# Three graphs of a batched graph network: earlier steps, turning by DMA, and two gathers in place of four

## The reference

```python
A = (adj != 0)
h = x
for l in range(5):
    m = h @ weight[l]
    agg = einsum('bij,bid->bjd', A, m)
    h = gru_cell(agg, h, w_ih, w_hh, b_ih, b_hh)
x = layernorm(x + h * mask)
fused = 0
for g, idx in enumerate(GROUPS):          # 25, 9, 7, 6 and 6 nodes
    h = graph_conv(x[:, idx], adj[:, idx][:, :, idx], W1[g], b1[g])
    fused[:, idx] += norm_w[g] * graph_conv(h, ..., W2[g], b2[g])
x = layernorm(x + fused)
```

## Time and profile before

| What | Value |
|---|---|
| Median of three executions | 503.38 us |
| The profiled execution's own time | 503.91 us |
| Its span, from first to last instruction | 502.2 us |
| PE busy | 486.9 us, 97% of the span |
| DVE, POOL, ACT busy | 75%, 63%, 59% |
| Mean granted TensorE clock | 0.995 of full speed |

### The profile page before, as it was taken

How to read it: one execution, slowest core, us unless ns; L and a number is a source line. 1 busy time by engine, 2 the same in 40 slices (tenths; PEclk the granted TensorE clock), 3 DMA queues, 4 the chain that set the end, 5 groups by cost and what they waited for, 6 DMA issues and landing times.

```text
span 502.2 us, 7158 instructions
## 1 busy us (share of the span) xinstructions
PE 486.9 (97%) x2313; PEld 230.8 (46%) x2313; DVE 375.8 (75%) x711; ACT 297.1 (59%) x522; POOL 318.6 (63%) x314
## 2 busy tenths in 40 slices
PE   7999999999999999999999999999989999999994
PEld 4344444444444444444444444434434444564564
DVE  3867867697857688998789878878664878545795
ACT  4546655645565666666567665566653656745564
POOL 3654775758775687776696567869652546324465
PEclk9999999999999999999999999999998999999999
DMA  8768253665525357345937565352242331322313
GB/s 276 229 166 170 44 151 66 175 114 152 146 44 168 84 120 175 83 84 124 209 72 180 146 145 146 64 104 45 42 103 43 63 69 42 63 61 43 78 44 85
DMA packets 131620, 55.44 MB, mean 110 GB/s; under 512 B 95145, under 2 KB 123262, under 8 KB 131582
## 3 DMA queue, kind: packets, MB, share of 16 engines
q1 hardware_dynamic: 106204, 31.86, 30.9%
q10 hardware_dynamic: 25378, 23.12, 15.2%
HBM read 27.70 MB, written 4.19 MB: 64 GB/s over the span
## 4 chain that ended last, share of the span: by engine, by line
PE 78%; DVE 11%; ACT 3%; issue 2%; DMA 2%; POOL 2%; SPq 1%; POOLq 0%; ACTq 0%; DVEq 0%
PE pA L757 23%; PE pR L764 6%; PE pR L762 6%; PE pR L763 6%; PE pZ L764 6%; PE pZ L763 6%; PE pZ L762 6%; PE pHN L762 3%; PE pHN L763 3%; PE pHN L764 3%; PE pIN L762 3%; PE pIN L764 3%; PE pIN L763 3%; DVE T L1354 2%; DVE T L1358 2%
## 5 line engine op out<-in xcount | busy, mean ns | idle before, releaser
L757 PE MATMUL pA<-A,NAT 128*128 128x512 fp8e4 x640 | 152.7, 381 | 0.6 <-DMA NAT<-HT 0.3
L520 POOL TENSOR_TENSOR HT<-H,HT 128x512 f16<-128x512 f32 x74 | 89.1, 1205 | 100.3 <-ACT HT L1126 100.0
L509 POOL TENSOR_TENSOR ZH<-Z,H 128x512 f32<-128x512 f32 x80 | 102.8, 1286 | 38.4 <-ACT Z L1139 36.9
L1354 DVE SCALAR_TENSOR_TENSOR T<-pHN,BHN,R 128x512 f32<-128x512 f32 x80 | 59.9, 749 | 70.8 <-ACT R L1132 70.5
L1143 ACT ACTIVATE pIN<-T,COLS 128x512 f32<-128x512 f32 x80 | 55.4, 692 | 76.3 <-DVE T L1358 76.2
L757 PEld LDWEIGHTS pA<-A,NAT 128*128 128x128 f16 x640 | 62.4, 98 | 76.5 <-issue 1.9
L1126 ACT ACTIVATE HT<-H 128x512 f16<-128x512 f32 x74 | 46.7, 631 | 63.3 <-DVE H L1367 63.2
L1363 DVE SCALAR_TENSOR_TENSOR pIN<-Z,pIN 128x512 f32<-128x512 f32 x80 | 55.1, 689 | 22.5 <-ACT pIN L1143 22.4
L1132 ACT ACTIVATE R<-pR,BRZ 128x512 f32<-128x512 f32 x80 | 54.5, 681 | 27.7 <-PE pR L764 27.1
L1349 DVE TENSOR_TENSOR AG<-pA,AG 128x512 f16<-128x512 f32 x80 | 54.7, 684 | 9.6 <-ACT AG L1122 9.6
L1367 DVE TENSOR_TENSOR H<-ZH,pIN 128x512 f32<-128x512 f32 x80 | 54.9, 687 | 4.2 <-POOL ZH L509 1.6
(11 more groups left out here) (282 smaller groups left out, 832.3 us busy)
## 6 DMA issues: line engine op xcount, KB each, us to landing
AS<-in_adj_dram ACTq DMA_DIRECT2D x13, 1024.0 KB, 6.1
XR<-in_x_dram ACTq DMA_DIRECT2D x16, 256.0 KB, 2.9
XS<-in_x_dram ACTq DMA_DIRECT2D x13, 256.0 KB, 3.2
out_dram<-Y SPq DMA_DIRECT2D x16, 192.0 KB, 2.2
AS<-in_adj_dram SPq DMA_DIRECT2D x2, 1024.0 KB, 8.7
AS<-in_adj_dram SPq DMA_DIRECT2D x4, 256.0 KB, 6.0
NAT<-HT SPq DMA_TRANSPOSE x64, 3.1
XS<-in_x_dram SPq DMA_DIRECT2D x3, 256.0 KB, 7.7
```

Source lines behind the costliest of these rows:

```text
L509: g_.tensor_tensor(ZH[:, :], Z[:, :], H[:, b, :], ALU.mult).then_inc(zh_p, 1)
L520: g_.tensor_tensor(HT[:, b, 1, :], H[:, b, :], HT[:, b, 0, :], ALU.subtract).then_inc(h_lo, 1)
L757: last = mm(pA2[:, k % 2, :], NAT[:, k % 2, h, i, :], A8[:, b, i, :], start=(h == 0 and i == 0), stop=(h == 1 and i == NI - 1))
L1354: v.scalar_tensor_tensor(out=T[:, :], in0=pHN[:, :], scalar=BHN[:, 0:1], in1=R[:, :], op0=ALU.add, op1=ALU.mult).then_inc(t_v, 1)
```

## The change

`ROUNDS` lists the steps in another order from step 55 on, `BY_DMA` is 12 in place of 10, POOL gathers groups 1 and 2 at iteration 59 and 3 and 4 at iteration 60, "prep" and "A01" stand one iteration earlier, and at iteration 76 `state_lo` stands ahead of `early_messages` on POOL. `E0` (the first graph of the last four) is 12 as before.

```diff
-          (11, 10, 12, 8, 9, 13, 14, 15),
-          (11, 10, 12, 9, 11, 13, 14, 15),
-          (10, 11, 12, 13, 14, 15),
+          (11, 10, 12, 8, 9),
+          (11, 10, 13, 9),
+          (11, 10, 14, 15),
+          (11, 12, 13, 14, 15),
+          (12, 13, 14, 15),
           (12, 13, 14, 15),
           (12, 13, 14, 15)]
...
-BY_DMA = 10
+BY_DMA = E0 = 12
...
-BATCH_AT = {"prep": (63, 0), "A01": (65, 0), "A2": (71, 1), ...
+BATCH_AT = {"prep": (62, 0), "A01": (64, 0), "A2": (71, 1), ...
...
-                elif 59 <= k < 59 + G - 1:
-                    g, j = k - 58, 0
-                    dst = BDA[:, :, P + SLOT[g - 1]:P + SLOT[g]]...
-                    for run in runs_of(GROUPS[g]):
-                        last = g_.tensor_copy(dst[:, :, :, j:j + len(run)], BD[:, g, 0:TAIL, :, run[0]:run[-1] + 1])
-                        j += len(run)
+                elif 59 <= k < 61:
+                    for g in ((1, 2), (3, 4))[k - 59]:
+                        j = 0
+                        dst = BDA[:, :, P + SLOT[g - 1]:P + SLOT[g]]...
+                        for run in runs_of(GROUPS[g]):
+                            last = g_.tensor_copy(dst[:, :, :, j:j + len(run)], BD[:, g, 0:TAIL, :, run[0]:run[-1] + 1])
+                            j += len(run)
...
                 if k == BATCH_AT["sum"][0] + 1:
                     inverse_roots_batch()
+                if SPLIT[k - 1] and k >= EARLY - 2:
+                    state_lo(k - 1)
                 if EARLY - 2 <= k + 1 < K - 1:
                     early_messages(k + 1)
...
-                if SPLIT[k - 1]:
+                if SPLIT[k - 1] and k < EARLY - 2:
                     state_lo(k - 1)
```

More of the change, by code:

```diff
@@ L84 @@
 WIDE = P + PACK
-BATCH_AT = {"prep": (63, 0), "A01": (65, 0), "A2": (71, 1), "B0": (72, 0), "B1": (72, 1), "S": (73, 0),
+BATCH_AT = {"prep": (62, 0), "A01": (64, 0), "A2": (71, 1), "B0": (72, 0), "B1": (72, 1), "S": (73, 0),
             "T": (73, 1), "D": (74, 0), "sum": (75, 0)}
@@ L97 @@
 EARLY = K - 2
-E0 = Q * TAIL
+assert E0 == Q * TAIL
 ROWS_OF = [S if max(m) >= S // 2 else S // 2 for m in GROUPS]
@@ L566, in prepare_batch @@
                     g_.tensor_copy(BDA[:, :, 0:P].rearrange("p c (q n) -> p c q n", q=Q), BD[:, 0, 0:TAIL, :, :])
-                elif 59 <= k < 59 + G - 1:
-                    g, j = k - 58, 0
-                    dst = BDA[:, :, P + SLOT[g - 1]:P + SLOT[g]].rearrange("p c (q j) -> p c q j", q=Q)
-                    for run in runs_of(GROUPS[g]):
-                        last = g_.tensor_copy(dst[:, :, :, j:j + len(run)], BD[:, g, 0:TAIL, :, run[0]:run[-1] + 1])
-                        j += len(run)
+                elif 59 <= k < 61:
+                    for g in ((1, 2), (3, 4))[k - 59]:
+                        j = 0
+                        dst = BDA[:, :, P + SLOT[g - 1]:P + SLOT[g]].rearrange("p c (q j) -> p c q j", q=Q)
+                        for run in runs_of(GROUPS[g]):
+                            last = g_.tensor_copy(dst[:, :, :, j:j + len(run)], BD[:, g, 0:TAIL, :, run[0]:run[-1] + 1])
+                            j += len(run)
                     if g == G - 1:
```

## The result

| | Kernel before | Changed kernel |
|---|---|---|
| Median, us | 503.75 (six executions, 501.49 to 505.07) | 497.75 (six, 497.40 to 498.51) |
| Profiled execution, us | 503.91 | 498.51 |
| Its span, us | 502.2 | 496.8 |
| PE busy, us | 486.9 | 484.0 |

The ratio is 0.9887, with a 95% interval of 0.9862 to 0.9913: 1.1% faster. The executions also lie closer together, within 1.1 us where those of before spread over 3.6 (in a later job the changed kernel spread over 1.7).

What follows compares the result with a forecast made beforehand. PE, busy in 97% of the span, was taken to bound the kernel by its work, waits and low-clock stretches. 503.91 - 0.86 - 2.02 - 1.70 - 1.35 + 0.40 = 498.4 us, range 497.2 to 501.6.

Steps and rivals of the forecast that it cites:

- The gather: PE's wait at "prep" for POOL's last gather goes, minus 2.02 us, with 2.0 us left between gather and "prep".
- The clock: The stretch at clock 0.50 behind the wait at "prep", 377.3 to 380.7 us, goes with that wait: minus 1.7 us.
- the clock falls anyway: Rival: the low-clock stretch comes even without the wait at "prep", 500.1 us; chance 0.14.
- Iteration 54: PE's wait at pIN for DVE's new state goes, as POOL no longer slows two scaling operations: minus 1.35 us.
- Turning by PE: The four PE transposes each of graphs 10 and 11 go, replaced by DMA transposes: minus 0.86 us.
- The new wait: At pIN of iteration 63, batch matrices plus graph 9's statistics take 2.89 us of DVE time: plus 0.4 us.
- The middle taken for iterations 64 and 66: Extra DVE work of 1.0 + 0.86 and 1.0 + 1.14 us gives no wait; with the longest times, 0.36 and 1.12.
- the rule: A VectorE instruction with two SBUF inputs and a GpSimd one reading SBUF block each other; 0.3 us more on the upper bound.
- The rest at nothing: Moved first splits and states (iterations 58 to 60), iteration 76's low half and later copies cost PE zero.
- DVE's waits: Rival: iteration 54's wait stays (1.35 us) and the new waits reach their bound (1.5 more), 501.3 us; chance 0.17.
- no turned state was late: Rival: a DMA transpose landing in 6.8 us in place of 3.0 holds PE 3.8 us, 502.2 us; chance 0.04.
- the finishing work: Rival: finishing graphs 9 to 11 crowds DVE, PE losing 1.35 us in each of iterations 62 to 67, 506.1 us; chance 0.05.

Runs made afterwards that it cites:

- wait made longer again: Kernel before, with PE's two "prep" transposes ahead of its wait for the last gather and two more small POOL copies ahead of that gather: 503.12 us.
- the first four experiments: Gathers put back in the changed kernel (501.09 us); in the kernel before, gathers moved (500.24), graph 15's cast one iteration later (502.06), both edits (499.67).
- with the statistics ahead: Changed kernel with DVE's batch matrices three iterations later and one graph's statistics ahead of another's scaling operations: 496.24 us.

## Why the prediction was right

- **The gather, 2.02 us: right.** The wait is gone in the changed kernel and in the kernel before with this edit alone; putting it back brings 1.9 us of idle time. The margin was said to be 2.0 us and is 1.9.
- **The clock, 1.70 us: right in size, and incomplete in its reason.** The prediction said that the low stretch follows the wait. In the four traces where PE is idle for 1.86 us (before), 1.89 (gathers put back), 1.86 (cast one iteration later) and 1.91 (wait made longer again), a stretch at 0.50 or 0.51 follows; with 1.59 us, and in the traces of the changed kernel and of the kernel before with its gathers moved, none does. The rival "the clock falls anyway" is out for this place. What the text lacked: by the times, the stretch does not come in every execution. That fits the two groups of times of the kernel before on two of the chips (on the chip of the first four experiments its 14 executions, 501.70 to 504.86, show no gap), and the smaller spread of the changed kernel. The forecast took all of the 1.70 from one execution that had the stretch, 503.91 us. That the later median, 503.75, was so close to it is luck: beside the last wait experiment the same kernel had a median of 502.43.
- **Iteration 54, 1.35 us: right.** -1.36 by PE's starts. The added POOL operation shows the cause that was read from the earlier trace rows. The reading was short in one point: the first state slows the first scaling operation only, and the 1.16 us of the second stand beside the split that follows on POOL at 325.38.
- **Turning by PE, 0.86 us: right in size, the account was short.** The starts give -0.88. The other way of finishing costs more than its transposes once two graphs' scalings meet, as the kernel with graph 11 on PE shows; in the kernel before they didn't meet.
- **The new wait, +0.40: right in place, measured 0.34.** The room of 2.48 us held: 2.83 us (374.89 to 377.72) were used. The middle taken for iterations 64 and 66, nothing, is what came; the extra DVE work there was 1.85 and 1.65 us. The masks of graphs 10 and 11, for which the rule was weighed, took 0.68 and 0.69 us; no POOL operation of 128x512 stood beside them.
- **The rest at nothing: right**, tested by itself for the low half of iteration 76 alone. That the burst of first splits in iterations 58 to 60 is hidden shows in the trace: PE has no wait between 327 and 379 us.
- **The sum.** From the aggregation of step 54 (iteration 53) to that of 79 the trace gives -5.61 us, the prediction's terms -5.53. The start of the profiled execution was 0.66 us later by then, and the end 0.45 us shorter. The start is not the change's, since the programs are the same there. Nor is the end by PE's work: from the aggregation of step 79 to the issue of the last store both take 23.22 us, and the 0.45 lie behind it (3.9 and 3.5 us). All eight traces with the new order have the short end, but of the six with the old order two have it too. Two ends of the forecast's own range were added up wrong: with the new waits at their bound of 1.9 in place of 0.4 it is 499.9 (not 500.3), and without them and at the median 497.5 (not 497.3). Neither changes what was forecast.
- **The rivals.** DVE's waits did not grow, no turned state was late, and no iteration from 62 to 67 lost more than 0.34 us. That the finishing work can crowd an engine is real, though: it showed on ACT, with one graph turned the old way.

## What to carry to other kernels

Where PE is busy 97% of the time, write down for each other engine how much extra work fits between two of its operations that PE waits for (here 2.48 us of DVE work per iteration), and place side work by that room, not by the engine's total. Producers of a side stage should end in an iteration before the one that uses them: one gather behind an operation that itself waits for PE cost 2.0 us, and 3.7 in the executions with a low stretch, and one changed line and a regrouped loop took it away. Before an order of steps is rewritten, try the single moves alone: on the old order they gave all but 0.5 us of PE's time in its steps.

## What was not expected of the hardware

A little more idle time changed what the clock did. With 1.59 us idle, none of ten executions takes more than 502.85 us; with 1.91 us, eight of twelve lie about 2 us above the other four, and the two profiled ones fit this. That a low stretch stands behind each of the eight is inferred, since only one has a trace. Their mean granted clocks agree with one exception: the four traces with the stretch have 0.994 or 0.995 for the whole execution and the ten without it 0.997 to 0.999; of the eight, seven have 0.994 or 0.995 and one 0.997, and the other four have 0.997 or 0.998. The two kernels ran on different chips, but on each the kernel before, with 1.86 us idle, shows both groups. The stretches at 0.50 (1.2 GHz) last about 3.4 us here and begin 0.6 to 1.7 us after PE is back at work. Small operations on DVE pay for POOL out of proportion: 0.15 us becomes 1.23 when a POOL operation of 1.72 us began 0.5 us before, and it ends when that one does (325.46 and 325.44; with the statistics ahead, 210.24 and 210.22).
